# Last layer's rows in fixed regions per expert, scattered in three groups; straight programs for two engines

## The chip, the cores and the metric

The kernel runs on one core of a Trainium2 chip. The metric is the device time of one execution in microseconds (us), the median of several runs. Each core has TensorE (matrix products, PE in the profile; PEld is its loading of weights), VectorE (DVE), ScalarE (ACT), GpSimd (POOL), SyncE (SP, used here as the loading queue) and 16 DMA engines. SBUF is the on-chip memory of 128 partitions, PSUM the memory that TensorE writes.

## The reference

Two transformer layers on x of shape (2, 512, 256), float32, with residual additions and normalizations between the parts. Layer 0 has an attention of 16 heads whose values come from a triangular solve, and a mixture of 64 experts with 8 of them per token and a capacity. Layer 1 has a linear attention (cumulative sums over windows of tokens) and a mixture of 8 experts, 2 per token:

```
logits = x @ gate_w.T;  p = softmax(logits);  top-2 experts and weights per token, weights sum to 1
y = (silu(x @ w1[e].T) * (x @ w3[e].T)) @ w2[e].T        for each of the token's two experts e
out = x_residual + sum over its two experts of weight * y
```

In layer 1 an expert takes however many tokens choose it.

## The kernel before

The 1024 tokens are 8 tiles of 128 rows (`NT = 8`). Each stage is a block in which every engine has a program of its own, and semaphores order them; an engine waits in its own order, so whatever stands behind a wait is late too.

**Layer 0's experts** (L1114 to L1366). GpSimd scatters the normalized rows to `expert_rows` in HBM with 64 indirect DMAs (L1304). The loading queue brings each expert's 256 rows back, TensorE turns them (L1140), projects (L1147), turns the hidden values (L1155) and projects down (L1164). ScalarE copies and applies silu (L1281, L1290, L1277), VectorE multiplies and copies (L1248, L1240). The helper `steps` runs two groups of eight experts as plain code, five in a hardware loop, and the last as plain code, on each engine.

**Clearing.** During the attention of layer 0 the loading queue writes zeros to `expert_rows` (L1003) and to `sorted_rows` (L1036), the buffer of the last layer, before it waits for the attention (L1039).

**Layer 1 up to the selection** (L1445 to L1793). GpSimd gathers the outputs of layer 0's experts (L1853, 48 indirect DMAs), VectorE adds them up (L1694). The linear attention goes through four windows of two tiles: `features` on ScalarE (L1633 to L1639), `window` on VectorE (L1705 to L1712), `out_lin` on TensorE (L1501), `add_outputs` (L1719), `norm_ffn` (L129 to L137), the turning of the normalized rows (L1476, L1621) and `logits` (L1509). VectorE's `select` takes the top two of four tiles at a time: `select(0)` before the last window, `select(1)` after the last logits. The choice itself is there at L1758. ScalarE swaps its table between square root and exponential with `load_table` (L1617); the last load of the square root table stands before `turned_ffn(NQ - 2)`, the copy that the logits of tiles 4 and 5 wait for.

**Sorting.** Each token's rank within its expert is a running count over all tokens: products of a triangular matrix and of ones with the chosen-expert marks (`ranks`, L1516), and one product more for the totals (L1541). From the totals VectorE works out how many tiles of 128 rows each expert needs, the first row of each expert in a densely packed buffer (L1797 to L1803), and each token's row number, `slots` (L1805 to L1810). So no slot is known before the last token's logits. Then GpSimd scatters all 8 tiles twice, once for each of the two experts (L1868, 16 indirect DMAs), each row with its weight and a mark for its token. VectorE goes on to the list `owner`: which expert each tile belongs to (L1812 to L1817).

**The tile loop.** `TL = 1024 * 2 / 128 + 7 = 23` tiles are as many as can be needed. When all scatters have landed, the loading queue loads tile t to one of two buffers (L1451); TensorE turns it (L1555), reads the owner to a register and projects with that expert's weights (L1561), turns (L1571) and projects down (L1580); ScalarE copies (L1672) and applies silu (L1681); VectorE multiplies, copies and weighs (L1840, L1821, L1827); GpSimd adds the rows to the output in HBM with an indirect DMA (L1877). All engines run it by `tiles_by_four`: four tiles as plain code, 16 in a hardware loop, three as plain code.

```
sp.wait_ge(s_sc, 16 * K1 * NT)       # L1455: every scatter has landed
load(0, 0)
load(1, 1)
```

## Time and profile before

| | |
|---|---|
| runs before | 1086.72 us, median of 3 (1083.01 to 1089.64) |
| profiled execution | 1090.66 us, its span in the trace 1088.9 us |
| mean granted clock of TensorE | 0.812 of full |
| busy, share of the span | TensorE 66%, VectorE 51%, ScalarE 28%, GpSimd 23% |
| DMA | 130.09 MB, mean 119 GB/s |

A row of the page or of a view gives busy time and share; the timeline gives the start in us from the span's beginning, the duration, the engine and line, and in brackets the idle time before it and what ended it ("issue": nothing that the profile shows; "remote": another core or a queue or signal that it cannot name). The chain of waits is read as start, duration, what. A granted clock of 1.00 is 2.4 GHz, 0.50 is 1.2 GHz. Busy shares are means over stages with different limits, so the stretches have to be looked at one by one.

### The profile page before, as it was taken

The numbers are of one execution on the slowest core, as the hardware profiler recorded it, in microseconds if no ns is written. First come the engines' busy times: TensorE is split into PE (matmuls) and PEld (weight loads), VectorE is DVE, ScalarE is ACT, GpSimd is POOL, SyncE is SP. The second block draws the span as 40 slices with busy tenths as digits, with TensorE's granted clock in tenths as the row PEclk, the third lists the DMA queues.
The fourth block names the chain that finished last, engine by engine and source line by source line (L and its number), as shares of the span: only waits on it lengthen the run. The fifth ranks groups of instructions, "written<-read, shape, count | busy, mean of one in ns | idle before, by whom it ended". The sixth has DMA issues, their size and how long they took to land. (4 is left out here: it accounts for less than half of the span.)

```text
span 1088.9 us, 16871 instructions
## 1 busy us (share of the span) xinstructions
PE 713.9 (66%) x6082; PEld 528.3 (49%) x6127; DVE 559.4 (51%) x1633; ACT 309.2 (28%) x529; POOL 251.9 (23%) x258
## 2 busy tenths in 40 slices
PE   4867287587767848740116999999131662499995
PEld 2434264364454436540115999998121551266663
DVE  6977895985997772356001333333343763033332
ACT  1014224343543553210002444443021461111110
POOL 5002102111111110006771000003577202222222
PEclk9989698888978966955556999999556685699998
DMA  3960006405232801059534888887333102222220
GB/s 126 170 93 30 1 3 186 56 6 155 53 39 105 326 2 49 6 162 419 213 133 139 282 292 291 291 290 226 92 97 92 34 1 74 67 44 44 44 41 4
DMA packets 70932, 130.09 MB, mean 119 GB/s; under 512 B 12240, under 2 KB 35280, under 8 KB 69840
## 3 DMA queue, kind: packets, MB, share of 16 engines
q1 hardware_dynamic: 56288, 94.29, 29.6%
q0 software_dynamic: 10224, 21.12, 7.2%
q10 hardware_dynamic: 4352, 13.77, 3.3%
q8 instruction: 43, 0.70, 0.3%
q14 instruction: 25, 0.20, 0.1%
HBM read 75.27 MB, written 54.58 MB: 119 GB/s over the span
## 5 line engine op out<-in xcount | busy, mean ns | idle before, releaser
L1147 PE MATMUL scores<-wgu,zero 128*128 128x192 f32 x512 | 98.0, 336 | 8.3 <-issue 8.3
L655 DVE TENSOR_REDUCE block_maxima<-scores 128x10 f32<-128x1280 f32 x64 | 92.4, 1486 | 8.4 <-PE scores L354 7.4
L850 ACT ACTIVATE E<-scores 128x1280 f32<-128x1280 f32 x64 | 77.5, 1238 | 58.4 <-PE scores L365 32.5
L1248 DVE TENSOR_TENSOR val<-sel,scores 128x192 f32<-128x192 f32 x64 | 22.7, 354 | 138.4 <-ACT sel L1290 106.9
L1147 PEld LDWEIGHTS scores<-wgu,zero 128*128 128x128 f32 x512 | 85.4, 197 | 9.0 <-issue 9.0
L1304 POOL DMA_INDIRECT expert_rows<-xn_moe,scatter_slots x64 | 62.5, 977 | 115.0 <-DVE gather_slots L1224 95.8
L1561 PE MATMUL scores<-w,xgT 128*128 x184 | 88.6, 606 | 0.3 <-issue 0.3
L1140 PE MATMUL misc<-cf,xg 128*128 128x128 f32 x256 | 40.7, 284 | 54.5 <-issue 54.5
L1164 PE MATMUL scores<-wd,slot 96*128 96x256 f32 x256 | 68.8, 392 | 10.2 <-issue 10.2
L962 POOL TENSOR_SCALAR_AFFINE_SELECT E<-E 128x256 f32<-128x256 f32 x64 | 27.2, 449 | 206.9 <-ACT E L850 206.9
L1281 ACT COPY zero<-misc 128x512 f32<-128x512 f32 x64 | 37.5, 586 | 130.1 <-PE misc L1140 119.3
L1140 PEld LDWEIGHTS misc<-cf,xg 128*128 128x128 f32 x256 | 33.9, 147 | 61.0 <-issue 54.9
L1240 DVE COPY xnT<-scores 128x512 f32<-128x512 f32 x64 | 44.3, 692 | 35.9 <-PE scores L1164 33.0
L1853 POOL DMA_INDIRECT gb<-expert_outputs,gather_slots x48 | 54.8, 1141 | 30.6 <-DVE X L1694 17.1
L1877 POOL DMA_INDIRECT out<-yb,add_to x23 | 35.5, 1544 | 110.4 <-DVE yb L1827 108.4
L1315 POOL DMA_INDIRECT gb<-expert_outputs,gather_slots x16 | 16.4, 1024 | 180.8 <-DMA expert_outputs<-xnT 176.2
L354 PE MATMUL scores<-cb 128*128 128x128 bf16 x256 | 54.9, 235 | 1.9 <-issue 0.9
L1164 PEld LDWEIGHTS scores<-wd,slot 96*128 96x128 f32 x256 | 45.0, 196 | 14.9 <-issue 11.1
L730 DVE TENSOR_TENSOR tmp<-Y,LB 128x120 f32<-128x120 f32 (+35 forms) x244 | 50.5, 248 | 0.3
L739 DVE TENSOR_TENSOR Y<-Y,tmp 128x120 f32<-128x120 f32 (+35 forms) x244 | 50.4, 248 | 0.1
L419 PE MATMUL misc<-LB,E 32*32 32x32 f32 x512 | 17.6, 231 | 45.6 <-DVE LB L745 37.9
L868 ACT COPY XT<-turned 32x1024 f32<-32x1024 f32 x16 | 30.9, 1931 | 47.0 <-DVE turned L746 46.7
(246 smaller groups left out, 1495.5 us busy)
## 6 DMA issues: line engine op xcount, KB each, us to landing
expert_rows<-zero SPq DMA_DIRECT2D x32, 512.0 KB, 6.2
xg<-expert_rows SPq DMA_DIRECT2D x64, 256.0 KB
expert_outputs<-xnT SPq DMA_DIRECT2D x64, 256.0 KB
wgu<-in_wgu SPq DMA_DIRECT2D x32, 384.0 KB, 3.6
w<-in_w ACTq DMA_DIRECT2D x8, 1024.0 KB
wd<-in_wd SPq DMA_DIRECT2D x32, 192.0 KB, 3.7
w<-in_w ACTq DMA_DIRECT2D x8, 512.0 KB
xg<-sorted_rows SPq DMA_DIRECT2D x23, 136.0 KB, 2.1
```

The costliest lines, as they stand in the source:

```text
L354: ins = nc.tensor.matmul(scores[:, slot, o + w - P:o + w], identb, mask[c, it], start=False, stop=True)
L655: nc.vector.tensor_reduce(bm[:, c, h, :], scores[:, slot, 0:WIDE].rearrange("p (a n) -> p a n", n=P), AX.X, ALU.max).then_inc(s_fd, 1)
L730: nc.vector.tensor_tensor(part, Yc[:, x, 0:n, k:k + 1].to_broadcast([P, n, w]), LB[:, k:k + 1, k + 1:SB].to_broadcast([P, n, w]), ALU.mult ...
L739: nc.vector.tensor_tensor(below, below, part, ALU.add).then_inc(s_inv, 1)
L850: nc.scalar.activation(to[:, h, :], scores[:, k % 2, 0:WIDE], ACT.Exp, scale=SCALE).then_inc(s_fa, 1)
L1140: ins = nc.tensor.transpose(misc[:, j % 2, c:c + P], xg[:, j, t, k * P:(k + 1) * P], identf)
L1147: ins = nc.tensor.matmul(scores[:, j % 2, t * 2 * F0:(t + 1) * 2 * F0], xgT[:, j % 2, k, t * P:(t + 1) * P], wgu[:, j // GE, j % GE, k, :] ...
L1164: ins = nc.tensor.matmul(scores[:, j % 2, 1024 + t * D:1024 + (t + 1) * D], hT[:, j % 2, t * P:(t + 1) * P], wd[:, j // GE, j % GE, :], st ...
L1240: nc.vector.tensor_copy(yb[:, j % NY].rearrange("p t d -> p (t d)"), scores[:, j % 2, 1024:1536]).then_inc(s_yv, 1)
L1304: pool.indirect_dma_start(out=xbuf, out_offset=bass.IndirectOffsetOnAxis(ap=isc[:, t, k:k + 1], axis=0), in_=xn[:, t, :], in_offset=None, ...
L1561: ins = nc.tensor.matmul(scores[:, j, g * F1:(g + 1) * F1], xgT[:, j, k, :], w13[:, bass.ds(e, 1), k, g * F1:(g + 1) * F1].rearrange("p e ...
L1853: pool.indirect_dma_start(out=gb[:, g % NG, :], out_offset=None, in_=ybuf, in_offset=bass.IndirectOffsetOnAxis(ap=ig[:, t, k:k + 1], axis= ...
```

## The change

ScalarE and VectorE run layer 0's expert loop and the last layer's tile loop as plain code; TensorE keeps both loops, SyncE keeps the first. In the last layer each expert has a fixed region of 1024 rows, so a token's slot needs its rank alone and not the totals. Ranks, slots and scatters go in three groups: tiles 0 to 3, 4 and 5, 6 and 7. Where each of the 23 tiles lies is worked out from the totals (`rows_at`), and the loading queue reads it to a register for each load; there are four tile buffers instead of two. The ranks go to `misc`, the logits of tiles 4 and 5 too. The buffer of 65 tiles is cleared in 22 DMAs instead of 8.

```diff
-        xs = nc.dram_tensor("sorted_rows", [TL * P, RW], F32, kind="Internal").ap()
+        xs = nc.dram_tensor("rows_by_expert", [E1 * N + P, RW], F32, kind="Internal").ap()
+        TZ = (E1 * N + P) // P
+        NZ1 = -(-TZ // 3)
...
+            def all_steps(total, body):
+                for i in range(total):
+                    body(i, i == 0, i == total - 1)
...
-                    steps(dve.Fori, E0 // NB, body)
+                    all_steps(E0 // NB, body)
...
-                    steps(act.Fori, E0 // NB, body)
+                    all_steps(E0 // NB, body)
...
+            def logits_in(q):
+                return misc[:, 0, NT * E1:2 * NT * E1] if q == NQ - 2 else scores[:, 1, LG:LG + NT * E1]
...
-            token = sbf("token", [P, NT])
+            marks = sbf("marks", [P, NT + TL])
+            token, tile_row = marks[:, 0:NT], marks[:, NT:NT + TL]
...
-            GROUPS = (slice(0, NT // 2), slice(NT // 2, NT))
+            GROUPS = (slice(0, 4), slice(4, 6), slice(6, 8))
...
-            xg = sbf("xg1", [P, 2, RW])
+            xg = xl[:].rearrange("p t d -> p (t d)")[:, 0:4 * RW].rearrange("p (j d) -> p j d", j=4)
...
+                    sp.wait_ge(s_own, 1)
                     sp.wait_ge(s_sc, 16 * K1 * NT)
-                    load(0, 0)
-                    load(1, 1)
...
-                    tiles_by_four(sp.Fori, body)
+                    for t in range(TL):
+                        if t >= 4:
+                            sp.wait_ge(s_tw, t - 3)
+                        row = sp.value_load(rows_at[0:1, t:t + 1], min_val=0, max_val=E1 * N)
+                        sp.dma_start(xg[:, t % 4, :], xs[bass.ds(row, P), :]).then_inc(s_ld[t % 4], 16)
...
-                    def ranks(tiles):
-                        for t in tiles:
+                    def ranks(x):
+                        pe.wait_ge(s_sel, x + 1)
+                        for t in range(GROUPS[x].start, GROUPS[x].stop):
                             for q in range(t + 1):
-                                ins = nc.tensor.matmul(scores[:, 0, t * E1:(t + 1) * E1], triu if q == t else onesb,
+                                ins = nc.tensor.matmul(misc[:, 0, t * E1:(t + 1) * E1], triu if q == t else onesb,
                                                        selb[:, q, :], start=(q == 0), stop=(q == t))
-                        return ins
+                        ins.then_inc(s_rk, 1)
...
                         if q:
                             logits(q - 1)
+                        if q == NQ - 1:
+                            ranks(0)
                         out_lin(q)
+                    ranks(1)
                     turn(at_ffn(NQ - 1), xn, NQ - 1)
                     logits(NQ - 1)
 
-                    pe.wait_ge(s_sel, 1)
-                    ranks(range(NT // 2))
-                    pe.wait_ge(s_sel, 2)
+                    ranks(2)
                     for q in range(NT):
-                        nc.tensor.matmul(scores[:, 0, T:T + E1], onesb, selb[:, q, :], start=(q == 0), stop=(q == NT - 1))
-                    ranks(range(NT // 2, NT)).then_inc(s_rk, 1)
-                    pe.wait_ge(s_own, 1)
-                    pe.wait_ge(s_sl1, 1)
+                        ins = nc.tensor.matmul(scores[:, 0, T:T + E1], onesb, selb[:, q, :], start=(q == 0), stop=(q == NT - 1))
+                    ins.then_inc(s_rk, 1)
+                    pe.wait_ge(s_own, 2)
...
-                        load_table(ACT.Sqrt)
+                        if q < NQ - 1:
+                            load_table(ACT.Sqrt)
                     turned_ffn(NQ - 2)
+                    exp_probs(1)
+                    load_table(ACT.Sqrt)
                     std_of(at_ffn(NQ - 1), NQ - 1)
                     load_table(ACT.Exp)
                     turned_ffn(NQ - 1)
-                    exp_probs(1)
+                    exp_probs(2)
...
-                    tiles_by_four(act.Fori, body)
+                    for t in range(TL):
+                        body(t, t % 4)
...
+                    def slots_of(x):
+                        tiles, n = GROUPS[x], GROUPS[x].stop - GROUPS[x].start
+                        dve.wait_ge(s_rk, x + 1)
+                        rk = misc[:, 0, 0:NT * E1].rearrange("p (t e) -> p t e", e=E1)[:, tiles]
+                        link(nc.vector.tensor_tensor(pos[:, tiles], rk, region[:].unsqueeze(1).to_broadcast([P, n, E1]), ALU.add))
+                        for k in range(K1):
+                            ins = nc.vector.tensor_tensor(at_k[:, k, tiles], pos[:, tiles], one[:, k, tiles], ALU.mult)
+                        link(ins)
+                        link(nc.vector.tensor_reduce(slot_f[:, :, tiles], at_k[:, :, tiles], AX.X, ALU.add))
+                        nc.vector.tensor_copy(slots[:, :, tiles], slot_f[:, :, tiles]).then_inc(s_sl1, 1)
...
                     dve.wait_ge(s_lw, 16 * 8)
+                    link(nc.vector.tensor_scalar(region[:], iota8, float(N), -1.0, ALU.mult, ALU.add))
                     nc.vector.tensor_scalar(nbias[:], bias[:], -1.0, None, ALU.mult).then_inc(s_nb, 1)
...
                     window(NQ - 1, 1)
+                    slots_of(0)
+                    select(1)
                     add_outputs(NQ - 1)
                     norm_ffn(NQ - 1)
-                    select(1)
-
-                    dve.wait_ge(s_rk, 1)
+                    slots_of(1)
+                    select(2)
+                    slots_of(2)
+
+                    dve.wait_ge(s_rk, 4)
...
+                    link(nc.vector.tensor_scalar(skip[:], tiles[:], -float(P), float(N), ALU.mult, ALU.add))
+                    link(nc.vector.tensor_tensor(skipped[:], past[:], skip[0:1, :].unsqueeze(1).to_broadcast(tq), ALU.mult))
+                    link(nc.vector.tensor_reduce(rows_f[:], skipped[:], AX.X, ALU.add))
+                    link(nc.vector.tensor_tensor(rows_f[:], rows_f[:], tile_row[0:1], ALU.add))
+                    nc.vector.tensor_scalar(rows_at[:], rows_f[:], float(E1 * N), None, ALU.min).then_inc(s_own, 1)
...
-                    tiles_by_four(dve.Fori, body)
+                    for t in range(TL):
+                        body(t, t % 4)
...
-                    pool.wait_ge(s_rc, NQ)
-                    pool.wait_ge(s_sl1, 1)
                     pool.wait_ge(s_zf1, 16 * NZ1)
-                    for k in range(K1):
-                        for t in range(NT):
-                            pool.indirect_dma_start(
-                                out=xs, out_offset=bass.IndirectOffsetOnAxis(ap=slots[:, k, t:t + 1], axis=0),
-                                in_=rows1[:, k, t, :], in_offset=None, bounds_check=TL * P - 1,
-                                oob_is_err=True).then_inc(s_sc, 16)
+                    for x in range(3):
+                        pool.wait_ge(s_rc, 2 + x)
+                        pool.wait_ge(s_sl1, x + 1)
+                        for k in range(K1):
+                            for t in range(GROUPS[x].start, GROUPS[x].stop):
+                                pool.indirect_dma_start(
+                                    out=xs, out_offset=bass.IndirectOffsetOnAxis(ap=slots[:, k, t:t + 1], axis=0),
+                                    in_=rows1[:, k, t, :], in_offset=None, bounds_check=E1 * N - 1,
+                                    oob_is_err=True).then_inc(s_sc, 16)
```

## Rows read from the trace of the kernel before

**Rows 1.** The page, busy time and share of the span of TensorE.

```profile
PE 713.9 (66%) x6082; PEld 528.3 (49%) x6127; DVE 559.4 (51%) x1633; ACT 309.2 (28%) x529; POOL 251.9 (23%) x258
```

**Rows 2.** Busy time by stretch: length, PE, PEld, DVE, ACT, POOL (count), clock, DMA share, GB/s.

```profile
650.00:700.00 50.00, 50.00 (x321) 46.55 (x320) 18.63 (x36) 20.57 (x54) 0.00 (x0) 1.00 0.85 289
902.00:937.00 35.00, 3.86 (x56) 3.45 (x56) 7.69 (x46) 3.12 (x6) 15.87 (x16) 0.54 0.27 94
...
1000.00:1050.00 50.00, 50.00 (x188) 30.55 (x188) 17.10 (x44) 8.73 (x18) 13.86 (x9) 1.00 0.26 43
```

**Rows 3.** The chain of waits, pieces in order of time: start us, us, what.

```profile
816.57 15.61 another core or an unknown queue
...
893.65 1.28 ACT L1617
...
895.67 1.88 PE scores L1509 x8
...
902.05 35.09 issue
937.14 2.10 DMA xg<-sorted_rows
...
941.25 0.34 issue
941.59 5.79 PE scores L1561 x8
...
953.20 0.22 PE misc L1555 x2
...
959.01 0.22 PE misc L1555 x2
```

**Rows 4.** Timeline of VectorE, 896 to 915 us, from the last window to the slots.

```profile
896.40 0.42 DVE L1712 SCALAR_TENSOR_TENSOR ctxT<-cum,relu 128x256 f32<-128x256 f32 x1
...
901.66 0.75 DVE L129 BATCH_NORM_STATS2 stats<-X 128x6 f32<-128x256 f32 x2
...
907.29 0.19 DVE L1741 TENSOR_REDUCE mx<-scores 128x4 f32<-128x32 f32 x1 [3.30 <-PE scores L1509]
...
910.30 0.19 DVE L1758 TENSOR_TENSOR selb<-one 128x32 bf16<-128x32 f32 x1
...
911.72 0.17 DVE L1797 TENSOR_SCALAR counts<-scores 128x8 f32<-128x8 f32 x1 [0.74 <-PE scores L1516]
...
913.05 0.23 DVE L1805 TENSOR_TENSOR pos<-scores,first_slot 128x64 f32<-128x64 f32 x1
...
914.03 0.17 DVE L1810 CAST slots<-slot_f 128x16 uint32<-128x16 f32 x1
```

**Rows 5.** Timeline of GpSimd, the first and the last of the 16 scatters.

```profile
915.22 1.08 POOL L1868 DMA_INDIRECT sorted_rows<-rows_ffn,slots  x1 [55.45 <-issue]
...
934.67 0.99 POOL L1868 DMA_INDIRECT sorted_rows<-rows_ffn,slots  x1 [0.30 <-issue]
```

**Rows 6.** Timeline of the loading queue, the clearing and the next DMA behind it.

```profile
364.68 9.00 SPq L1036 DMA_DIRECT2D sorted_rows<-zero  x8
416.67 0.39 SPq L1039 DMA_DIRECT2D LB<-in_wo  x1
```

**Rows 7.** Timelines of VectorE and GpSimd, 779 to 839 us, additions and gathers.

```profile
779.82 6.81 DVE L1694 SCALAR_TENSOR_TENSOR X<-gb,w,X 128x256 f32<-128x256 f32 x17
...
782.68 4.84 POOL L1853 DMA_INDIRECT gb<-expert_outputs,gather_slots  x1 [0.30 <-DVE X L1694]
...
816.41 1.02 POOL L1853 DMA_INDIRECT gb<-expert_outputs,gather_slots  x1 [0.31 <-issue]
...
838.12 1.02 POOL L1853 DMA_INDIRECT gb<-expert_outputs,gather_slots  x1 [0.67 <-issue]
```

**Rows 8.** Waits from 560 to 800 us: us in total, times, longest.

```profile
ACT sel L1290 <- remote: 34.5, 3, 16.5
...
ACT slot L1277 <- remote: 7.5, 1, 7.5
```

More of the change, by code:

```diff
@@ L1427, in build_kernel @@
             s_own, s_sl1, s_sc = sem("owners_ready"), sem("slots1_ready"), sem("rows_scattered1")
-            s_ld = [sem("rows_loaded0"), sem("rows_loaded1")]
+            s_ld = [sem(f"rows_loaded{j}") for j in range(4)]
             s_xt, s_xc, s_g, s_u = sem("rows_turned1"), sem("rows_copied1"), sem("gate1_done"), sem("up1_done")
@@ L1590, in body @@
                         if not (isinstance(t, int) and t + 1 == TL):
[L1591 removed]
+                            turn_x(t + 1, (q + 1) % 4)
                         pe.wait_ge(s_xc, t + 1)
@@ L1736, in select @@
                         each = range(GROUPS[x].start, GROUPS[x].stop)
-                        dve.wait_ge(s_lg, (NQ // 2, NQ)[x])
+                        dve.wait_ge(s_lg, 2 + x)
                         b = [P, n, E1]
-                        lg = scores[:, 1, LG:LG + NT * E1].rearrange("p (t e) -> p t e", e=E1)[:, tiles]
+                        lg = logits_in(1 + x).rearrange("p (t e) -> p t e", e=E1)[:, tiles]
                         mxs, prs = mx[:, tiles], pr[:, tiles]
@@ L1801, in _ @@
                     link(nc.vector.tensor_tensor_scan(ends[:], onesf.to_broadcast([P, E1]), tiles[:], 0.0, ALU.mult, ALU.add))
-                    link(nc.vector.tensor_tensor(first_slot[:], ends[:], tiles[:], ALU.subtract))
-                    link(nc.vector.tensor_scalar(first_slot[:], first_slot[:], float(P), -1.0, ALU.mult, ALU.add))
-                    rk = scores[:, 0, 0:NT * E1].rearrange("p (t e) -> p t e", e=E1)
-                    link(nc.vector.tensor_tensor(pos[:], rk, first_slot[:].unsqueeze(1).to_broadcast(bc), ALU.add))
-                    for k in range(K1):
-                        ins = nc.vector.tensor_tensor(at_k[:, k], pos[:], one[:, k], ALU.mult)
-                    link(ins)
-                    link(nc.vector.tensor_reduce(slot_f[:], at_k[:], AX.X, ALU.add))
-                    nc.vector.tensor_copy(slots[:], slot_f[:]).then_inc(s_sl1, 1)
                     link(nc.vector.tensor_scalar(cnt[:], ends[:], float(CAP), None, ALU.mult))
@@ L1880, in _ @@
                             oob_is_err=False, compute_op=ALU.add).then_inc(s_ad, 16)
+                    pool.wait_ge(s_out, 16)
+                    for t in range(TL):
+                        add_to_output(t)
 def shape_constants():
@@ L1898, in shape_constants @@
                          np.tile(np.arange(E1), (P, 1)), np.ones((P, 1)), np.tile(np.arange(E0) * CAP, (P, 1)), ones2,
-                         N - np.arange(N).reshape(NT, P).T], 1).astype(np.float32)
+                         N - np.arange(N).reshape(NT, P).T,
+                         r[:, None] + P * np.arange(TL)[None, :]], 1).astype(np.float32)
     neg = -1e30
```

42 lines of the change are left out of this document (16 added, 26 removed).

## The prediction

> **What bounds the kernel now.** I read the page first. TensorE is busy 66% of the span, a mean over stages that have different limits [rows 1], so the next view is the busy time by stretch [rows 2]. In the expert loop of layer 0 (650 to 700 us) and in the tile loop of the last layer (1000 to 1050 us) TensorE is busy all of the time at the full clock, while VectorE has 18.6 and 17.1 us of work in 50 and ScalarE 20.6 and 8.7. Between 902 and 937 us TensorE works 3.9 us in 35 at a granted clock of 0.54, which is mostly its 1.2 GHz level, and GpSimd works 15.9. The chain of waits [rows 3] shows the same: from 902.05 to 937.14 us the loading queue only waits; then one load takes 2.10 us, and from there TensorE alone sets the end, 5.82 us per tile (953.20 to 959.01), 23 tiles.
>
> What fills the 35 us is in the timelines. VectorE starts the last normalization at 901.66, gets the last logits 5.6 us later at 907.29, has the selection of both experts at 910.49 (910.30 and 0.19), waits for the ranks until 911.72, and writes the row numbers ("slots") at 914.20 [rows 4]. GpSimd starts 1.0 us later: 16 scatters from 915.22 to 934.67, 15 steps of 1.30 us, and 0.99 for the last, so 935.66 [rows 5]. The first tile's load is issued 1.48 us later. So the path is: last logits, selection, ranks, slots (7 us), 16 scatters (20.4 us), their landing, load, tiles.
>
> **The change, part by part.**
>
> *Straight programs in the expert loop and the tile loop.* TensorE keeps its loops, and in both loops it is busy for 50 us of 50 [rows 2]. A shorter step of ScalarE or VectorE starts nothing sooner there. I take zero, covered by TensorE; without that cover the edit would be worth the register and branch work of these two engines, which no row shows. Bounds: upwards, some of the waits at the loop's entry and exit may belong to it (first rival); downwards, the programs grow, and nothing in the trace has a price for that except that VectorE and ScalarE have 31 and 29 us free in 50.
>
> *Fixed regions per expert.* The buffer grows from 23 to 65 tiles of 128 rows, so clearing it takes 22 DMAs for 8. Eight take 9.00 us on the loading queue from 364.68; 14 more take 15.8 and end at 389.5. The queue then waits until 416.67 in any case [rows 6], so 27 us of cover remain and I take zero. The added 5.9 MB would have to trail by those 27 us to cost anything, and no other load is issued in between. The extra operation for the regions' start stands before VectorE's first use of the biases, and the gathers wait for VectorE's additions after it: 0.2 us, all on the path.
>
> *Scatter in three groups.* I walk the path again with the same rows. The edit has a part that is easily overlooked: ScalarE's load of the square root table, 1.28 us at 893.65 and 0.2 for its dummy, goes behind the copy of the turned rows and the exponential, and that copy is what the logits of tiles 4 and 5 wait for (895.67, 1.88 us [rows 3]). They run from 894.2 to 896.1, and the ranks of tiles 0 to 3 behind them, ten small products, take 0.4. The last window ends at 896.8 (896.40 and 0.42). VectorE does the slots of group 0 from there. The five steps cost 1.15 us for eight tiles (913.05 to 914.20); I take 1.0 for four, so 897.85. The selection of tiles 4 and 5 follows. It took 3.2 us for four tiles up to the choice (907.29 to 910.49) and 0.5 behind it; half the tiles save four of the eight short search steps, so 2.6 and 0.45: 900.9. TensorE's products for the residual additions run from 896.9 to 900.6, so nothing waits, and after two additions (0.9) the normalization starts at 901.8; before it was 901.66. So the added VectorE work in front is paid by the earlier logits, and the last logits come at 907.4, hardly moved. The slots of group 1 fall into the wait for them. Selection of two tiles: choice at 910.0. Ranks of tiles 6 and 7 are 15 products for the 34 before: 0.6 us instead of 1.2. Slots of group 2: ready at 911.5, for GpSimd at 912.5.
>
> GpSimd can begin at 897.85 + 1.0 = 898.85. Group 0 keeps it busy to 909.2, group 1 (ready at about 906) to 914.4, and group 2 is ready 1.9 us before that. So **GpSimd is never idle**, and the end is its own: 898.85 + 15 x 1.297 + 0.99 = 919.3 us instead of 935.66. The order in three groups does not take 12 scatters off the path; it moves the whole row of 16 forward by 16.4 us.
>
> VectorE now works beside the scatters, and one row speaks against that: the gather issued at 782.68 took 4.84 us where others take 1.02, while VectorE ran 17 additions without a gap from 779.82 to 786.63 [rows 7]. Beside the shorter steps with links between them, which are what runs here, the gather at 816.41 took 1.02 next to a window's steps, and the one at 838.12 came 0.37 late (0.67 of idle time for 0.30) next to a normalization [rows 7]. I take 0.4, the nearest rows; the ends are 0 and 6.3 (no scatter progresses before VectorE pauses at about 905.1). The Trainium skill, "SBUF — State Buffer", section "SBUF: two separate sides", says that VectorE and GpSimd share a port pair as an exclusive lock, and that a DMA issued from GpSimd can wait for its descriptors while VectorE holds it. By that rule alone the sum would lose up to those 6.3 us; the 4.84 us row agrees with it, the 1.02 us rows beside VectorE's linked steps do not show it.
>
> *Tiles loaded at a register's row.* The wait for the row numbers hides: counts, tiles per expert, rows and owners are a dozen small VectorE steps of 0.2 to 0.4 us behind 911.5, done at about 915, before the last scatter. Each load adds one register read. No row shows it; TensorE, which reads the owner the same way, stood still 0.34 us ahead of its first product [rows 3]. I take 0.3, between 0.1 and 1.0. Later loads have 5.82 us each and four buffers instead of two.
>
> *The table load in its new place, wider constants.* It now ends at about 900, and the standard deviation is not wanted before 902. Zero, with 2 us of cover; without them 1.5. The wider load of the constants lies beside VectorE's first additions: zero.
>
> **The sum.** Load of the first tile: 919.3 + 0.4 + 1.48 + 0.3 = 921.5 instead of 937.14, 15.6 us earlier. From there nothing changes: 2.1 us of landing, the first products at the 1.2 GHz level (5.79 us [rows 3] for what takes 3.44 at full clock), then 5.82 per tile. [...] Minus 0.2 for the regions: **15.4 us**. The profiled execution took 1090.66 us around a span of 1088.9, so 1075.3; it lies 3.94 above the median of the three runs, 1086.72, against which the sum gives **1071.3 us**. On its own terms it can be 3 us to either side.
>
> **Rivals.**
>
> *The straight programs do more.* At the expert loop's entry and exit, and behind it, ScalarE stands still for signals of TensorE that should long be there: 34.5 us in three waits before L1290, 7.5 before L1277 [rows 8], then 15.61 on the chain [rows 3]. None falls inside the loops. If a loop's end makes them, part goes. Worth: 57.6 in all, less the longest at the entry, 16.5, beside which the scatters of layer 0 still set the pace, so 41 at most: 1030; half of it 1051. Against it: the engine that signals there is TensorE, whose loops stay. The Trainium skill, "Runtime: NRT & Kernel Launch", section "Instruction fetch mechanics", says that a taken branch can break the sequential prefetch and stall, and prefers unrolling; by that rule the time falls under this rival, and no row here ties one of the waits to a fetch. I give it 0.12.
>
> *A late signal takes some back.* All of these waits lie where GpSimd issues one indirect DMA after another or just after. Here that is now so from 899 to 920, with four TensorE signals on the path. One of 7.5 us, less the slack of 1.9, leaves 9.8 of 15.4 (1077); one of 15.6 leaves 1.7 (1085). 0.20.
>
> *GpSimd is held by VectorE* through the normalization: 6.3 for 0.4 us, 1077. 0.10.
>
> *Slower.* The same mechanism twice: late signals for the turned rows and for the last logits, each 15.6 us, on a path that before had GpSimd idle beside it. The path moves by 31.2 − 1.9 = 29.3, minus 15.4: 1101. It decides from 17.3 us of lateness in sum. For it: three in a row at the expert loop's entry; against it: it takes two of the longest kind, of which the chain of waits has one. 0.07.
>
> *The groups do not overlap*, because group 0 waits on something that I have not seen, as the clearing or the copies of the rows: all 16 scatters then start at 912.5, 2.7 us sooner than now, 1084. 0.03.
>
> **The numbers.** As summed: 0.48. Faster by over 0.5% (5.4 us, about what a measurement of this kernel can tell from no change) are the sum, the first rival, most of the held one and half of the late signal: 0.77. Within 0.5%: 0.15. Slower: 0.08. The range goes from 1055, which leaves out half of the first rival, to 1083, which leaves out the slower case and the longer half of the late signals.
>
> **What would show it.** Right: scatters from about 899, in one row of 16 without gaps, to about 920; the first load near 921.5; the last logits within 1 us of their old place; 5.82 us per tile; clearing done by 390 with the next wait of that queue still ending near 417. Wrong: a gap in GpSimd's row ahead of group 2 with ScalarE or VectorE waiting on TensorE; scatters longer than 1.1 us; a register read of over 1 us; the waits before L1290 gone or grown.

## The result and the profile after

The changed kernel takes 1069.13 us, median of 4 runs (1061.71 to 1074.25), against 1084.87 us (1083.00 to 1089.64) of the kernel before beside it: ratio 0.9869, 95% interval [0.9826, 0.9913]. So it is 9 to 19 us faster; forecast were 1071.3 us and a range of 1055 to 1083. The profiled execution took 1068.96 us around a span of 1067.1, against 1090.66 around 1088.9.

That pair of traces differs by 21.8 us of span, more than the medians do (15.7). Where it comes from is read from the same views as before. The page's busy time has hardly moved [rows 1]:

```profile
PE 717.5 (67%) x6126; PEld 525.6 (49%) x6127; DVE 563.0 (53%) x1659; ACT 309.9 (29%) x530; POOL 251.4 (24%) x258
```

Nor have the two full stretches of [rows 2]: TensorE is still busy for 50 us of 50 in both, and VectorE as plain code works 18.1 and 16.8 us there for 18.6 and 17.1.

```profile
650.00:700.00 50.00, 50.00 (x320) 46.55 (x319) 18.14 (x35) 20.75 (x54) 0.00 (x0) 1.00 0.87 293
...
1000.00:1050.00 50.00, 50.00 (x191) 31.09 (x190) 16.80 (x45) 8.23 (x17) 13.24 (x9) 1.00 0.17 28
```

VectorE's timeline answers to [rows 4]. The rows are the last step of the last window, the slots of groups 0 and 1, the last logits, the choice for tiles 6 and 7, the first and the last step of group 2's slots, and the row numbers of the tiles:

```profile
887.54 0.42 DVE L1722 SCALAR_TENSOR_TENSOR ctxT<-cum,relu 128x256 f32<-128x256 f32 x1
...
888.68 0.17 DVE L1753 CAST slots<-slot_f 128x8 uint32<-128x8 f32 x1
...
895.83 0.22 DVE L1753 CAST slots<-slot_f 128x4 uint32<-128x4 f32 x1
898.49 0.17 DVE L1762 TENSOR_REDUCE mx<-scores 128x2 f32<-128x16 f32 x1 [2.45 <-issue]
...
900.95 0.17 DVE L1779 TENSOR_TENSOR selb<-one 128x16 bf16<-128x16 f32 x1
...
906.95 0.17 DVE L1748 TENSOR_TENSOR pos<-misc,region 128x16 f32<-128x16 f32 x1 [5.35 <-remote]
...
907.67 0.17 DVE L1753 CAST slots<-slot_f 128x4 uint32<-128x4 f32 x1
...
910.66 0.31 DVE L1836 TENSOR_SCALAR rows_at<-rows_f 1x23 int32<-1x23 f32 x1
```

Two things stand out. The last window ends 8.9 us sooner than before (887.54 for 896.40), ahead of every part of the change that could move it. And ahead of the slots of group 2 VectorE waits 5.35 us for a signal: TensorE's last rank product started at 901.6, and VectorE goes on at 906.95. GpSimd's timeline, the first scatter, the twelfth to the thirteenth, and the last [rows 5], shows what that does:

```profile
889.81 1.08 POOL L1891 DMA_INDIRECT rows_by_expert<-rows_ffn,slots  x1 [40.96 <-DVE slots L1753]
...
904.10 0.98 POOL L1891 DMA_INDIRECT rows_by_expert<-rows_ffn,slots  x1 [0.30 <-issue]
908.71 0.98 POOL L1891 DMA_INDIRECT rows_by_expert<-rows_ffn,slots  x1 [3.63 <-DVE slots L1753]
...
912.58 0.99 POOL L1891 DMA_INDIRECT rows_by_expert<-rows_ffn,slots  x1 [0.30 <-issue]
```

The row of 16 has a gap of 3.63 us for 0.30. The chain of waits, in place of [rows 3]:

```profile
901.60 5.26 another core or an unknown queue
906.95 0.19 DVE pos L1748
...
912.58 2.46 DMA rows_by_expert<-rows_ffn,slots
915.11 0.47 SPq L1471
...
916.08 2.13 DMA xn_lin<-rows_by_expert
...
920.55 5.00 PE scores L1567 x8
```

The late signal is now on the path, and so is the register read of the loading queue (L1471): from the end of the last scatter (913.57) to the first load 2.51 us go by, against 1.48 before. So of the 21.8 us, 8.9 lie before the last window's end, 12.2 between it and the first load (28.54 us for 40.74), and 0.7 behind it, where the first products took 5.00 us for 5.79. The clearing behaves as forecast [rows 6]: it is done at 388.7. The queue's next DMA comes at 417.8, 1.1 us later than before, but so does the clearing's start (365.74 for 364.68).

```profile
365.74 22.99 SPq L1036 DMA_DIRECT2D rows_by_expert<-zero  x22
417.82 0.39 SPq L1039 DMA_DIRECT2D LB<-in_wo  x1
```

Two questions stay: are the first 8.9 us the change's, and what is the late signal.

### The profile page after: what moved, and what is told of

Same layout as the page of the kernel before. It is cut to its first block and busy times, and to the rows that moved or that the text cites. A ratio compares the mean times of both kernels' runs of the same rounds, so it can differ in the third digit from the quotient of the medians.

```text
span 1067.1 us, 16859 instructions
## 1 busy us (share of the span) xinstructions
PE 717.5 (67%) x6126; PEld 525.6 (49%) x6127; DVE 563.0 (53%) x1659; ACT 309.9 (29%) x530; POOL 251.4 (24%) x258
## 5 line engine op out<-in xcount | busy, mean ns | idle before, releaser
L1320 POOL DMA_INDIRECT gb<-expert_outputs,gather_slots x16 | 16.4, 1025 | 177.0 <-DMA expert_outputs<-xnT 172.5
L1295 ACT ACTIVATE sel<-scores 128x192 f32<-128x192 f32 x64 | 21.2, 331 | 82.4 <-PE scores L1152 42.9
```

## The experiments

All kernels are measured against the kernel before on the same chip; they ran on four chips. The first pair's chip isn't on record; its signals are late as on B, C and D, and it counts with them below. Beside that pair, the changed kernel itself ran on chip A alone. The distance that tells most is from the start of the last window's last step on VectorE (ctxT) to the first tile's load, since nothing of the execution's earlier history is in it. All of it from the traces, in us; the last two columns are worked out from the rows:

| kernel | ratio [95%] | chip | ctxT | first scatter | last scatter's end | first load | ctxT to load | load to end of span |
|---|---|---|---|---|---|---|---|---|
| before, first trace | | | 896.40 | 915.22 | 935.66 | 937.14 | 40.74 | 151.8 |
| after, first trace | 0.9869 [0.9826, 0.9913] | | 887.54 | 889.81 | 913.57 | 916.08 | 28.54 | 151.0 |
| straight_only | 0.9985 [0.9969, 1.0] | A | 859.13 | 877.94 | 898.34 | 899.82 | 40.69 | 151.8 |
| loops_back | 0.9845 [0.9819, 0.987] | A | 863.65 | 865.92 | 886.31 | 888.83 | 25.18 | 151.0 |
| one_go | 0.9972 [0.9957, 0.9987] | A | 859.85 | 875.88 | 896.28 | 898.81 | 38.96 | 151.9 |
| after_again | 0.9844 [0.982, 0.9868] | A | 859.14 | 861.40 | 881.78 | 884.31 | 25.17 | 151.1 |
| before_again | 1.0005 [0.9985, 1.0025] | B | 886.09 | 904.91 | 925.36 | 926.84 | 40.75 | 151.8 |
| more_clearing | 1.0015 [0.9991, 1.004] | B | 893.87 | 912.69 | 933.08 | 934.57 | 40.70 | 152.5 |
| hoisted | 0.988 [0.9844, 0.9917] | B | 884.31 | 886.58 | 910.31 | 911.94 | 27.63 | 151.6 |
| table_first | 0.9916 [0.9886, 0.9947] | B | 893.61 | 896.99 | 920.74 | 923.24 | 29.63 | 152.3 |
| one_go_again | 0.9994 [0.9961, 1.0027] | C | 893.38 | 909.90 | 930.29 | 932.81 | 39.43 | 151.3 |
| ranks_by_sum | 0.9887 [0.9843, 0.9931] | C | 895.88 | 898.15 | 918.66 | 921.46 | 25.58 | 153.4 |
| sum_only | 0.9871 [0.9835, 0.9906] | D | 890.34 | 892.61 | 913.05 | 915.56 | 25.22 | 150.9 |
| no_gathers | single execution | D | 861.20 | 863.48 | 887.16 | 889.68 | 28.48 | 147.3 |

The kernel before took 1055.14 us in the median on chip A, 1084.82 on B, 1082.99 on C, 1081.38 on D. No trace from A has a wait of over 1.5 us for a TensorE signal that the profile can't name; every other trace has them.

**straight_only**: the kernel before with ScalarE's and VectorE's plain code alone.

```diff
-                    steps(dve.Fori, E0 // NB, body)
+                    all_steps(E0 // NB, body)
...
-                    tiles_by_four(dve.Fori, body)
+                    for t in range(TL):
+                        body(t, t % 4)
```

(and the same two on ScalarE).

> The kernel before with only the straight programs of ScalarE and VectorE in the two loops. Theory A (the row of scatters moved forward is the whole gain; straight programs are worth nothing): ratio 0.995 to 1.005, the waits of ScalarE for TensorE's signals near the expert loop and behind it as scattered as before, the first tile's load 20 us behind the first scatter as before. Theory B (the 8.9 us that the changed kernel had gained before the last window come from the straight programs): ratio near 0.992, about 9 us faster, and the last window's end near 888 us.

Measured: 1053.82 us, ratio 0.9985. The interval reaches from 0.3% faster to no change.

**loops_back**: the changed kernel with those four loops put back.

> The changed kernel with the hardware loops of ScalarE and VectorE put back in both places. Theory A: the same as the changed kernel, 0.987 of the kernel before, within 0.004. Theory B: 9 us of the gain are lost, ratio near 0.995.

Measured: 1038.66 us, ratio 0.9845, beside 0.9844 for the changed kernel itself. On chip A the plain code is worth nothing that can be measured, from both sides. But the first rival speaks of waits for late signals, and chip A has none, so these two runs can't refute it by themselves; no run on another chip changes the plain code alone. What the other traces show speaks against it. Off chip A, VectorE's first addition behind layer 0 starts at 775.9 to 779.8 us in the three traces with loops (before, before_again, more_clearing) and at 776.9 to 783.1 in the seven with plain code, and the waits before the `sel` copy ([rows 8]; L1295 in the kernels with plain code) come to 26 to 41 us with loops and 20 to 43 with plain code. And one_go_again below, plain code on chip C, is at most 4.2 us faster than the kernel before by its interval, 1.3 us of which its own stage shows (39.43 us from ctxT to load for 40.74). The 20 to 41 us that the first rival puts on the straight programs don't fit with that; a few us are not excluded. The Trainium skill, "Runtime: NRT & Kernel Launch", section "Instruction fetch mechanics", prefers unrolling because a taken branch can stall; this case's runs on chip A show no gain from it (0.9985 and 0.9845 for 0.9844) in loops in which TensorE is busy for 50 us of 50.

**one_go**: the changed kernel, its scatters held back until all slots are there.

```diff
                     pool.wait_ge(s_zf1, 16 * NZ1)
+                    pool.wait_ge(s_sl1, 3)
```

> The changed kernel, but GpSimd waits for the slots of all three groups before its first scatter, so nothing of it lies beside the selection. Theory A: the 16 scatters start about 1 us after the last slots and take 20.4 us; the late signal behind the ranks of tiles 6 and 7 (5.3 us in the changed kernel) is gone if scatters beside it cause it, so the last slots come near 903.5 on the changed kernel's clock, the scatters end near 925 and the first load is issued near 927 instead of 916: 11 us slower than the changed kernel, ratio 0.997. If the signal is late all the same, 5 us more, ratio 1.002.

Measured: 1052.11 us, ratio 0.9972, as theory A has it. Since no signal is late on chip A, the run says nothing on the late one. **after_again** is the changed kernel itself:

> The changed kernel once more, for a second trace on the same chip as the others. Theory A: ratio 0.987 within 0.004; the last window ends within 10 us of 888 and varies with how late TensorE's signals come, since nothing in this stretch is changed; the last scatter of group 2 again waits for slots if the signal of the last ranks is late, and not if it is on time. Theory B: the last window ends near 888 again.

Measured: 1039.22 us, ratio 0.9844. The last window doesn't end within 10 us of 888, as was expected, but 28 us sooner: without late signals the whole stretch ahead of it is shorter. The timeline on GpSimd (first and last scatter) and on VectorE (last window, group 0's slots, ranks arrived and slots of group 2) beside that of straight_only and one_go:

```profile
861.40 1.07 POOL L1891 DMA_INDIRECT rows_by_expert<-rows_ffn,slots  x1 [22.40 <-DVE slots L1753]
...
880.80 0.98 POOL L1891 DMA_INDIRECT rows_by_expert<-rows_ffn,slots  x1 [0.30 <-issue]
```

```profile
859.14 0.42 DVE L1722 SCALAR_TENSOR_TENSOR ctxT<-cum,relu 128x256 f32<-128x256 f32 x1
...
860.28 0.17 DVE L1753 CAST slots<-slot_f 128x8 uint32<-128x8 f32 x1
...
873.44 0.17 DVE L1748 TENSOR_TENSOR pos<-misc,region 128x16 f32<-128x16 f32 x1 [0.25 <-PE misc L1525]
...
874.16 0.17 DVE L1753 CAST slots<-slot_f 128x4 uint32<-128x4 f32 x1
```

straight_only, GpSimd's first and last scatter:

```profile
877.94 1.07 POOL L1875 DMA_INDIRECT sorted_rows<-rows_ffn,slots  x1 [38.94 <-issue]
...
897.36 0.98 POOL L1875 DMA_INDIRECT sorted_rows<-rows_ffn,slots  x1 [0.30 <-issue]
```

one_go, GpSimd's first scatter:

```profile
875.88 1.07 POOL L1892 DMA_INDIRECT rows_by_expert<-rows_ffn,slots  x1 [36.16 <-DVE slots L1753]
```

Here, without late signals, the change is seen bare. The last window ends at the same time in straight_only and after_again (859.13, 859.14), so nothing is gained ahead of it. The row of scatters starts 16.54 us sooner, has no gap (20.38 us from 861.40 to 881.78, as the 20.40 of straight_only), and the load comes 15.51 us sooner. one_go shows that this is the overlap and not the fixed regions: with the slots from ranks alone but no overlap, and with the 1.03 us of the register read, the load stands 38.96 us behind the last window's step where straight_only has 40.69, only 1.7 us sooner.

**before_again** is the kernel before, unchanged.

> The kernel before, unchanged, for its trace beside the others and for the noise of the comparison: ratio 1.000. Theory: the signals of TensorE that came 4 to 16 us late in the first trace of it (at 561, 571, 584, 765, 832 us) belong to the chip of that trace and not to the kernel. Then this trace, if it comes from the chip of the last runs, has no wait of over 1.5 us for a signal that the profile cannot name, its last window's VectorE work ends near 860, its first load is near 900 and its time near 1055. Rival: only the changed kernel and its relatives are free of them, so that the change itself removes them: then the waits of 3 to 16 us are here again and the last window ends some 30 us later.

Measured: ratio 1.0005. It ran on chip B, not A, so its time isn't the expected one; the signals are late here as in the first trace. straight_only, which is nearly the kernel before, has none on chip A, and the changed kernel has them on chips B and D, so they go by the chip and not by the change. Its trace answers the first question in another way: its last window ends at 886.09, 10.3 us sooner than in the first trace of the same kernel and sooner than in the changed kernel's first trace.

```profile
886.09 0.43 DVE L1712 SCALAR_TENSOR_TENSOR ctxT<-cum,relu 128x256 f32<-128x256 f32 x1
```

From VectorE's first addition to there, the traces with late signals take 103 to 117 us and those of chip A 92 to 95, before and after the change alike. So the 8.9 us belong to the executions that were profiled.

**more_clearing**: the kernel before with the large buffer and its 22 clearing DMAs.

```diff
-        xs = nc.dram_tensor("sorted_rows", [TL * P, RW], F32, kind="Internal").ap()
+        xs = nc.dram_tensor("sorted_rows", [(E1 * N + P), RW], F32, kind="Internal").ap()
...
```

> The kernel before, but with its buffer of sorted rows as large as the changed kernel's (65 tiles of 128 rows, of which 23 are used) and cleared as there, in 22 DMAs for 8. Theory (the prediction's step): the clearing ends at about 389 us and is covered by the queue's wait that ends near 417, so nothing moves: the time of the kernel before within 0.3%. Rival: 5.9 MB more of writes hold up transfers of the attention beside them, or wait for them, for up to 5 us: ratio up to 1.005, and a part of what the changed kernel gains by its scatters is lost there again.

Measured: 1088.58 us, ratio 1.0015 [0.9991, 1.004]. The loading queue's clearing and its next DMA:

```profile
366.00 22.81 SPq L1037 DMA_DIRECT2D sorted_rows<-zero  x22
417.66 0.39 SPq L1040 DMA_DIRECT2D LB<-in_wo  x1
```

The cover holds. On chip A, from the clearing's start to this next DMA it is 51.96 us with 8 clearing DMAs (straight_only, 364.80 to 416.76) and 51.99 with 22 (after_again, 364.84 to 416.83). A cost of up to 0.4% isn't excluded by the interval; in this stage the traces show no place for one.

**hoisted**: the register reads of the first four loads moved ahead of the wait for the scatters.

```diff
+                    rows = [sp.value_load(rows_at[0:1, t:t + 1], min_val=0, max_val=E1 * N) for t in range(4)]
                     sp.wait_ge(s_sc, 16 * K1 * NT)
...
-                        row = sp.value_load(rows_at[0:1, t:t + 1], min_val=0, max_val=E1 * N)
+                        row = rows[t] if t < 4 else sp.value_load(rows_at[0:1, t:t + 1], min_val=0, max_val=E1 * N)
```

> The changed kernel, but the loading queue reads the first four row numbers to registers ahead of its wait for the scatters, not behind it. After the last scatter's end the first load took 2.51 us in the changed kernel (913.57 to 916.08) and 2.52 in its second trace, against 1.47 and 1.48 where no register is read. Theory: the read and the address worked out from it cost 1.0 us, and they are on the path only because they stand behind the wait. Then the first load follows the last scatter's end by about 1.5 us and the time falls by 1.0 us against the changed kernel (0.9990 of it; on the chip of the last runs 1038.2 us). Rival: the 1.0 us belongs to a DMA whose address comes from a register, wherever the register is read. Then the load still follows by 2.5 us and the time is the changed kernel's.

Measured: 1071.03 us, ratio 0.988 [0.9844, 0.9917]. GpSimd's last scatter and the loading queue's first load:

```profile
909.32 0.99 POOL L1892 DMA_INDIRECT rows_by_expert<-rows_ffn,slots  x1 [0.30 <-issue]
```

```profile
911.94 1.92 SPq L1473 DMA_DIRECT2D xn_lin<-rows_by_expert  x4
```

The load follows by 1.63 us instead of 2.51: the theory holds in the trace, 0.9 of the 1.0 us is the read's place behind the wait, 0.15 stays with the address from a register. In the time, where single executions spread over 11 us, 0.9 us can't be seen.

**table_first**: the square root table's load back in front of the turned copy.

```diff
-                        if q < NQ - 1:
-                            load_table(ACT.Sqrt)
+                        load_table(ACT.Sqrt)
```

> The changed kernel with ScalarE's load of the square root table (1.28 us and 0.2 for its dummy) back in front of the copy of the turned rows of tiles 4 and 5; the second load, which the changed kernel has behind the exponential, stays. Theory (the prediction's credit): that copy is on the path to the first slots; the logits, the ranks of tiles 0 to 3, the first slots, all 16 scatters and the first load come later, by 1.4 us if nothing else gives way, by 0.9 if VectorE's last window, which in the changed kernel ends 0.8 us after the ranks could, takes the rest. So 0.9 to 1.4 us slower than the changed kernel. Rival: ScalarE's copy waits for something else there, and the moved load was worth nothing: the changed kernel's time within 0.3 us, first scatter at its place.

Measured: 1076.98 us, ratio 0.9916 [0.9886, 0.9947]. ScalarE loads the table ahead of the copy, and VectorE then waits for the ranks of tiles 0 to 3:

```profile
890.86 1.28 ACT L1623 ACT_TABLE_LOAD   x1
892.15 0.20 ACT L1623 ACTIVATE unused<-eps 128x1 f32<-128x1 f32 x1
892.26 0.57 ACT L1627 COPY xnT<-misc 128x512 f32<-128x512 f32 x1
```

```profile
895.05 0.19 DVE L1747 TENSOR_TENSOR pos<-misc,region 128x32 f32<-128x32 f32 x1 [1.02 <-PE misc L1525]
```

The first scatter stands 3.38 us behind the last window's last step instead of 2.27, the load 29.63 instead of 28.54: the moved load is worth 1.1 us on the path, within the expected 0.9 to 1.4. The last logits come 12.52 us behind that step (906.13) for 10.95 in hoisted on the same chip. The credit of the prediction is real, and it is one that only a walk over every instruction of the moved block finds.

**ranks_by_sum** and **sum_only** go after the late signal. TensorE makes 15 products for the ranks of tiles 6 and 7 and 8 for the totals, one after the other. VectorE has 2.5 us free before; it adds up the marks of tiles 0 to 5 there, and 5 and 3 products do. ranks_by_sum has the reads of hoisted as well, sum_only has this edit alone.

```diff
+                            first = GROUPS[x].start if x == 2 else 0
+                            if x == 2:
+                                nc.tensor.matmul(misc[:, 0, t * E1:(t + 1) * E1], onesb, selsum[:, 0, :], start=True, stop=False)
-                            for q in range(t + 1):
+                            for q in range(first, t + 1):
...
-                    for q in range(NT):
...
+                    nc.tensor.matmul(scores[:, 0, T:T + E1], onesb, selsum[:, 0, :], start=True, stop=False)
+                    for q in range(6, NT):
...
+                        link(nc.vector.tensor_reduce(selsum[:, 0, :], selb[:, 0:6].rearrange("p t e -> p e t"), AX.X, ALU.add))
                     select(2)
```

> The kernel with the first four register reads moved ahead, and in it TensorE's last products before the slots of tiles 6 and 7 are fewer: VectorE adds the marks of tiles 0 to 5 while it waits for the last logits, and TensorE makes the ranks of tiles 6 and 7 from 5 products for 15 and the totals from 3 for 8. In three traces of the changed kernel and its relatives on the chip where signals come late, the signal after these 23 products came 4.7 to 5.3 us late, and GpSimd stood still for 3.3 us ahead of its last four scatters. Theory A: TensorE falls behind there because it has many instructions at once to take in; with 8 products it does not, VectorE's wait ahead of the slots of tiles 6 and 7 is under 1 us, GpSimd has no gap, and the time falls by a further 3.3 us (ratio to before about 0.984). Theory B: something holds TensorE's signals up, however few products stand before them: the wait of about 5 us stays and so does the gap of 3.3 us (ratio about 0.987). On a chip without late signals there is nothing to win: the path runs over GpSimd, and only the 1.0 us of the register reads is gained, ratio 0.9835.

Measured: 1073.62 us, ratio 0.9887 [0.9843, 0.9931]; theory A's 0.984 was missed.

> The changed kernel with the fewer products alone (ranks of tiles 6 and 7 from 5 products for 15, totals from 3 for 8, VectorE adding up the marks of tiles 0 to 5), its register reads where the changed kernel has them. In the first trace with fewer products the signal was on time and GpSimd's row had no gap, but one trace is no proof against chance. Theory A (the 23 products in a bunch make TensorE fall behind beside the scatters): again no wait of over 1 us ahead of the slots of tiles 6 and 7, the 16 scatters in one row of 20.4 us; from the last window's end to the first load 26.5 us as on the chip without late signals, not 29.9. Rival (chance): the wait of about 5 us is back. The time hangs on what the rest of the execution loses before that: ratio to before 0.983 to 0.990 by A, 0.987 to 0.993 by the rival.

Measured: 1068.86 us, ratio 0.9871 [0.9835, 0.9906]. sum_only on VectorE (ranks of group 2 arrived, their slots, then the totals), and on GpSimd (twelfth, thirteenth and last scatter):

```profile
904.55 0.17 DVE L1754 TENSOR_TENSOR pos<-misc,region 128x16 f32<-128x16 f32 x1
...
905.28 0.17 DVE L1759 CAST slots<-slot_f 128x4 uint32<-128x4 f32 x1
906.14 0.17 DVE L1831 TENSOR_SCALAR counts<-scores 128x8 f32<-128x8 f32 x1 [0.69 <-remote]
```

```profile
906.90 0.98 POOL L1899 DMA_INDIRECT rows_by_expert<-rows_ffn,slots  x1 [0.30 <-issue]
908.19 0.99 POOL L1899 DMA_INDIRECT rows_by_expert<-rows_ffn,slots  x1 [0.30 <-issue]
...
912.06 0.99 POOL L1899 DMA_INDIRECT rows_by_expert<-rows_ffn,slots  x1 [0.30 <-issue]
```

In both kernels the wait for the ranks is gone and GpSimd has no gap: 25.22 us from the last window's step to the load, as on chip A (25.17), where the changed kernel has 28.54. The 3.3 us are won back in this stage. (sum_only's expectation counts from a step that starts 1.3 us sooner: its 26.5 us are 25.2 here, its 29.9 are 28.5.) Ahead of the totals VectorE still waits 0.69 us for something that the profile can't name; the changed kernel's trace on chip A has no wait there. That the time falls by 3.3 us isn't shown: the changed kernel didn't run on chips C and D, the intervals are 4 us to either side, and the signals that are late elsewhere (6.2 us at 827 in sum_only's trace, 11.2 us at 838 in before_again's) move single executions by more. ranks_by_sum, which was to beat the changed kernel by 4.2 us, has 25.58 us there for the 24.3 that both edits should give, and its ratio is not told from the changed kernel's in the first pair. What it gives back is in two places that were not expected. VectorE writes the row numbers 5.05 us after the slots (910.79 to 915.84), where hoisted takes 2.99, standing still between its own steps; and the register reads, now ahead of the wait, take 4.7 us, from 916.54 to 921.2, for 2.4 in hoisted. VectorE in ranks_by_sum:

```profile
914.45 0.33 DVE L1843 TENSOR_REDUCE rows_f<-skipped 1x23 f32<-1x184 f32 x1 [1.06 <-DVE skipped L1842]
...
915.84 0.24 DVE L1845 TENSOR_SCALAR rows_at<-rows_f 1x23 int32<-1x23 f32 x1 [0.85 <-DVE rows_f L1844]
```

The chain of waits of ranks_by_sum runs over these reads and no longer over the scatters:

```profile
916.54 0.53 SPq L1468
...
918.64 0.70 issue
919.35 0.70 SPq L1468
920.05 0.70 issue
```

"issue" is time in which the loading queue waited for nothing recorded.

**one_go_again** is one_go on a chip with late signals.

> The changed kernel with GpSimd waiting for the slots of all three groups before its first scatter, once more. Theory A: signals of TensorE come late only while GpSimd issues indirect DMAs or just after. From the last gather to the first scatter GpSimd now issues none, so on a chip with late signals the ones up to the last window are here as before, but VectorE waits under 1 us for the ranks of tiles 6 and 7, and the slots of group 2 are there 1.6 us after the choice. Theory B: the products of the ranks are late by themselves: the wait of about 5 us stands here too, and the first scatter comes that much later. In both cases most of what the change gains is gone, since all 16 scatters stand behind the last slots: ratio to before 0.997 by theory A, 1.001 by theory B.

Measured: 1085.62 us, ratio 0.9994 [0.9961, 1.0027], which holds both theory A's 0.997 and theory B's 1.001, so the time doesn't decide; the trace does. The ranks of tiles 6 and 7, 15 products, with GpSimd idle beside them:

```profile
908.00 0.17 DVE L1748 TENSOR_TENSOR pos<-misc,region 128x16 f32<-128x16 f32 x1 [0.25 <-PE misc L1525]
```

0.25 us of waiting, as on chip A, while VectorE waits 4.7 to 5.4 us for the same products in the four traces off chip A in which scatters run beside them (after, hoisted, table_first, no_gathers). The kernel before agrees: its 34 products, with GpSimd idle, are waited for 0.74 us in all three of its kind off chip A (before, before_again, more_clearing). Theory A holds, with one gap: the 23 products beside scatters didn't run on chip C.

**no_gathers**: the changed kernel without all but the first gathers of layer 0's expert outputs.

```diff
-                        dve.wait_ge(s_gb[g % NG], 16 * (g // NG + 1 + levels(g % NG)))
+                        if g < NG:
+                            dve.wait_ge(s_gb[g % NG], 16 * (g // NG + 1 + levels(g % NG)))
...
-                    for g in range(NG, NT * K0):
...
```

> The changed kernel without the 48 gathers of layer 0's expert outputs beyond the first ones, and without VectorE's waits for them. Left out: the right values of the sum over layer 0's experts; VectorE adds what lies in its buffers. Theory A: TensorE's late signals between 815 and 860 us come only with indirect DMAs issued beside. Without them no signal is late there by over 1.5 us, and the last window ends as on the other chip or sooner, some 29 us after its place now or earlier less what VectorE no longer waits. Theory B: they come from TensorE's own program in the linear attention: waits of 4 to 20 us stay though GpSimd is idle.

Measured, in a single execution: 1038.7 us. Not one signal is late between the end of layer 0 and the last window, which ends at 861.20, 29 us before sum_only's on the same chip. From VectorE's first addition to there it takes 82 us where sum_only takes 113; some 10 of these 32 are VectorE's waits for gathers that are gone too, since chip A takes 92 with all gathers and no late signal. (The tokens take other experts here, so nothing behind the first load is compared.) Those beside layer 0's scatters stay (15.2, 10.2 and 21.1 us among them), and so does the one of 4.68 us ahead of group 2's slots:

```profile
880.55 0.17 DVE L1749 TENSOR_TENSOR pos<-misc,region 128x16 f32<-128x16 f32 x1 [4.68 <-remote]
```

## Why the prediction was right, point by point

- **Straight programs, 0.** Right on chip A: 0.9985, and 0.9845 for 0.9844. Elsewhere a gain of a few us isn't excluded.
- **Regions' extra operation, 0.2 on the path.** No run isolates it.
- **Clearing, 0, covered.** Right: done at 388.7 (forecast 389.5).
- **Group 0's slots 1.0 us after the last window.** 0.9 (859.56 to 860.45).
- **Last logits hardly moved.** Right, where no signal is late: 870.08 and 870.03 us on chip A with equal starts. It holds because of the moved table load: with it back in its old place the last logits come 1.6 us later and the first slots 1.1.
- **Group 2 ready in time, GpSimd never idle, row 16.4 us forward.** 16.54 on chip A. In the result's trace the slots came 5.1 us late (a wait of 5.35 for 0.25), and 3.3 of that reached GpSimd: the rival "a late signal takes some back" came true within the forecast's result. Its rule for the place (while or just after GpSimd issues indirect DMAs) held off chip A; what it lacked is the number of products, and that a chip can be free of such signals.
- **VectorE holds GpSimd, 0.4 between 0 and 6.3.** 0. All 16 scatters take 0.98 to 1.08 us and follow each other by 0.30, though VectorE runs selection and normalization beside them. The lock that the Trainium skill describes in "SBUF — State Buffer", section "SBUF: two separate sides", doesn't show in this stage.
- **Register read, 0.3 between 0.1 and 1.0.** Mis-sized: 1.03 (2.51 for 1.48), just beyond its upper end. The nearest row taken was TensorE's 0.34 of "issue", which held no read ahead of a DMA with a computed address. The two errors of 0.4 too much and 0.7 too little nearly cancel: 15.5 measured for 15.6.
- **From the load on, nothing but the moment at which the clock rises.** 151.0 us for 151.8; the first products took 5.00 for 5.79, within the 3 us that the sum leaves to either side.

The forecast of 1071.3 us lies 2.2 above the median; 1.9 of that is the kernel before, 1086.72 when it was forecast from and 1084.87 beside the result. That 15.4 stands so close to the 15.7 between the medians is in part luck: with the late signal its own working gives 12.2 us of gain (15.4, less 5.1 of lateness, plus 1.9 of slack), and only the interval (9 to 19) holds both. Chip A, with 15.9 us, has the sum's case as it stands.

## What to carry to other kernels

A row of DMAs that has to be issued one by one is moved forward as a whole when its first group can start early; what counts is that every later group is ready before the engine gets to it, so look for the group's slack and for whatever is late just then. Cost a moved block by each instruction in it, and put reads of registers ahead of the wait, not behind. Where two traces of one pair differ by more than the medians, measure from an anchor just ahead of the changed stage: the traces here spread by 37 us at the last window, and from there to the first load those of the kernel before lie within 0.1 us, the changed kernel's at 25.2 or 28.5.

## What the runs showed of the hardware

On chips B, C and D and in the first pair TensorE's signals are waited for up to 22 us beside or just behind GpSimd's indirect DMAs, on chip A in none of four traces; the kernel before is 26 to 30 us faster there. The same lengths come back on different chips: a wait of 21.11 us in six traces, from all of B, C, D and the first pair. For the place in question, and off chip A, the conditions are told apart: 23 small products with scatters beside were late in 4 of 4 traces, 23 without scatters in 0 of 1 and 34 without in 0 of 3, and 8 with scatters in 0 of 2. On chip A 23 with scatters beside were on time in 2 of 2. VectorE and the loading queue stand still in the same stage at times without any recorded cause (the 0.70 us above). Instructions that reach an engine late would fit with that, but it isn't shown. The Trainium skill, "Runtime: NRT & Kernel Launch", section "Instruction fetch mechanics", says that each engine's sequencer fetches its instructions in blocks over a DMA queue of its own, mostly hidden behind those it executes. The page of the profile has two queues of this kind (packets, MB, share of 16 engines):

```profile
q8 instruction: 43, 0.70, 0.3%
q14 instruction: 28, 0.23, 0.1%
```

The chips can't be told apart by them: the changed kernel has these same two rows in its first trace and on chip A. And in the changed kernel's first trace, from 554 to 575 us, while ScalarE waits 21.11 us, the queues that moved anything are these two:

```profile
q0 software_dynamic: 775, 2.13, 27.8%
q1 hardware_dynamic: 288, 0.52, 8.5%
```

Nor does a packet of an instruction queue lie between 901.6 and 906.9, ahead of group 2's slots. So these two waits aren't tied to a fetch under way; whether one was asked for late, the record doesn't say. Other waits have a packet near them: the one of 13.7 us from 827.6 in the same trace starts behind a q8 packet at 826.9. The cause beneath the conditions stays open, and so does what sets chip A apart.
